# Two chosen-token layers with half of the rank comparisons, a moved gather and mask, and newly written orders for the last layer

## The reference, cut to what matters

```python
scores = jnp.einsum('btd,d->bt', hidden_states, w_router)
_, idx = jax.lax.top_k(scores, k)            # k = 128 of 1024
idx = jnp.sort(idx, axis=-1)
sel = hidden_states[b, idx]
x, pos = sel.reshape(S, D), idx.reshape(S)
...                                          # rms norm, q, k, v with biases, rope at pos
att = jnp.where(causal[None], att, jnp.finfo(att.dtype).min)
att = jax.nn.softmax(att, axis=-1)
...                                          # output projection, rms norm, gated MLP
gated = gate * processed + (1.0 - gate) * x  # gate = sigmoid(score)
output = hidden_states.at[b, idx].set(gated.reshape(B, k, D))
```

## Time and profile before

| | |
|---|---|
| median of 3 runs | 1503.42 us (1502.92 to 1507.25) |
| profiled execution, its own time | 1500.55 us |
| its span, first to last instruction | 1499.0 us |
| mean granted TensorE clock | 0.985 |
| PE busy | 1432.7 us (96%) |
| DVE, ACT, POOL busy | 1089.7, 1030.0, 680.9 us |
| f1 in the span | about 597 to 680 us |
| f2 | about 1147 to 1230 us |
| layer1 | about 1230 to 1499 us |

### The profile page before, as it was taken

The page is one execution under the profiler, slowest core; times in us unless marked ns, Lnnn a source line. Parts: engine busy times, 40 slices in busy tenths (PEclk is TensorE's granted clock), DMA queues, the critical chain, the costliest instruction groups (busy, mean ns, idle before and its releaser), DMA issues. The chain is left out here.

```text
span 1499.0 us, 23651 instructions
## 1 busy us (share of the span) xinstructions
PE 1432.7 (96%) x8460; PEld 1217.9 (81%) x8460; DVE 1089.7 (73%) x2447; ACT 1030.0 (69%) x2254; POOL 680.9 (45%) x816
## 2 busy tenths in 40 slices
PE   7899999999999998998999999999999997988899
PEld 6789898888989886786888888888897785766677
DVE  6989898989898976656766666766666749567643
ACT  4898989999898986465755655655654446675654
POOL 6676776676776555113433333343321112722233
PEclk9999999999999999999999999999999999899999
DMA  2000000000000000601000000000003314000000
GB/s 74 2 18 1 19 9 12 1 19 19 1 8 2 14 1 12 256 1 51 22 22 8 22 29 8 22 29 15 1 8 130 138 31 167 1 0 0 1 0 28
DMA packets 14339, 45.11 MB, mean 30 GB/s; under 512 B 3216, under 2 KB 3216, under 8 KB 12048
## 3 DMA queue, kind: packets, MB, share of 16 engines
q1 hardware_dynamic: 14224, 43.61, 8.1%
HBM read 42.55 MB, written 1.05 MB: 29 GB/s over the span
## 5 line engine op out<-in xcount | busy, mean ns | idle before, releaser
L386 POOL TENSOR_SCALAR a_prob<-a_prob,a_rowinv 128x128 f32<-128x128 f32 (+7 forms) x256 | 189.0, 753 | 132.1 <-DVE a_rowinv L380 131.9
L411 DVE TENSOR_TENSOR a_pT_lo<-ps,a_pT_hi 128x512 fp32r<-128x512 f32 (+3 forms) x384 | 194.8, 551 | 21.1 <-ACT a_pT_hi L403 19.4
L364 DVE CUSTOM_DVE_ANT_0 a_prob<-ps,a_mask 128x128 f32<-128x128 f32 (+7 forms) x256 | 187.0, 750 | 21.2 <-PE ps L149 20.9
L371 ACT ACTIVATE a_prob<-a_prob,a_negmax 128x128 f32<-128x128 f32 (+7 forms) x256 | 197.3, 778 | 2.2 <-DVE a_negmax L364 1.3
L386 POOL TENSOR_SCALAR b_prob<-b_prob,b_rowinv 128x128 f32<-128x128 f32 (+7 forms) x128 | 94.6, 751 | 199.6 <-DVE b_rowinv L380 199.5
L403 ACT ACTIVATE a_pT_hi<-ps 128x512 fp32r<-128x512 f32 (+3 forms) x384 | 167.3, 492 | 24.7 <-PE ps L344 15.4
L344 PE MATMUL ps<-ident,a_prob 128*128 128x128 f32 x1152 | 160.2, 275 | 7.0 <-DVE a_pT_lo L411 5.6
L371 ACT ACTIVATE b_prob<-b_prob,b_negmax 128x128 f32<-128x128 f32 (+7 forms) x128 | 99.6, 779 | 72.6 <-DVE b_negmax L364 71.8
L344 PEld LDWEIGHTS ps<-ident,a_prob 128*128 128x128 f32 x1152 | 130.0, 140 | 20.6 <-POOL a_prob L386 7.9
L149 PE MATMUL ps<-a_k_hi,a_q 128*128 128x512 f32 (+3 forms) x384 | 140.4, 373 | 1.9 <-DVE a_negmax L364 1.0
L355 PE MATMUL ps<-a_pT_hi,a_v 128*128 128x512 f32 (+3 forms) x384 | 131.2, 349 | 1.1 <-DVE a_pT_lo L411 0.6
(11 more groups left out here) (452 smaller groups left out, 4025.0 us busy)
## 6 DMA issues: line engine op xcount, KB each, us to landing
f_wq<-in_f_wq SPq DMA_DIRECT2D x2, 2048.0 KB, 9.0
f_wo<-in_f_wo SPq DMA_DIRECT2D x2, 2048.0 KB, 17.1
b_w_raw<-in_b_qk SPq DMA_DIRECT2D x16, 256.0 KB, 2.7
a_w_raw<-in_a_w SPq DMA_DIRECT2D x8, 384.0 KB, 3.2
a_vo<-in_a_o SPq DMA_DIRECT2D x8, 256.0 KB, 2.7
f_wk<-in_f_wk SPq DMA_DIRECT2D x2, 1024.0 KB, 10.8
f_wv<-in_f_wv SPq DMA_DIRECT2D x2, 1024.0 KB, 12.9
f_wg<-in_f_wg SPq DMA_DIRECT2D x2, 1024.0 KB, 19.7
```

The lines of the kernel that those rows point to most:

```text
L364: dve.tensor_tensor_reduce(slot(a, u), g.ps_flat[:, bank * HALF:bank * HALF + width], a.mask[:, N - width:], -1.0, -MASKED, ALU.add, ALU.m ...
L371: act.activation(prob, prob, ACT.Exp, bias=a.negmax[:, n:n + 1], scale=-1.0, accum_out=a.rowsum[:, n:n + 1]).then_inc(*g.exped.mark(a.tag, u))
L386: pool.tensor_scalar(prob, prob, a.rowinv[:, n:n + 1], 1.0, ALU.mult, ALU.mult).then_inc(*g.normed.mark(a.tag, u))
L411: dve.tensor_tensor(lo, src, fr(hi), ALU.subtract).then_inc(*g.lo.mark(a.tag, u, j0 // 4))
```

## The change

In `ffn`, a token of an early block is no longer compared with the blocks before it. Of a pair of tokens in different blocks one comparison is kept, and for blocks 0 to 4 (`F_ROWS` is 5) the missing count is worked out as the number of later tokens less the sum of the row, which ACT makes with accumulating copies (`held`); DVE subtracts and adds it to the ranks. The unread products become fewer (3, 2, 2, 2, 2, 1, 1, 0). The gather goes to bank 3 and runs between the products of `take` and `place`. The mask moves ahead of the rope factors. In the second half, the product for the gate goes ahead of `scores(2)`, `turn_prob(0)` ahead of `scores(3)`, and `turn_take` behind `out(3)`. Two of the copies of `h_tok` on ACT go behind the new copies. POOL gets an iota and two memsets more. In `layer1` the four strings are new; the steps are the same ones, counted by program.

```diff
+F_SPIN = (3, 2, 2, 2, 2, 1, 1, 0)
+F_ROWS = 5
+        f.unread = f.sq[:, :].rearrange("p b k q -> p (b k q)").bitcast(BF16)
...
-    pool.memset(f.upper[:], 1.0).then_inc(*done.mark(tag, "ones"))
+    pool.memset(f.lower[:], 1.0).then_inc(*done.mark(tag, "ones"))
+    pool.iota(f.later[:, 0:F_ROWS], pattern=[[-P, F_ROWS]], base=N - P, ...)
+    pool.memset(f.later[:, F_ROWS:TT], 0.0)
+    pool.memset(f.minus_b[:], -1.0)
...
 def ffn_beats(f, e, j):
-    own, hi = f.s_col[:, j:j + 1], (j + 1) * P
-    e.tensor_scalar(f.beats[j // 4][:, j % 4, 0:hi], f.s[:, 0:hi], own, None, ALU.is_lt)
-    if hi < N:
-        e.tensor_scalar(f.beats[j // 4][:, j % 4, hi:N], f.s[:, hi:N], own, None, ALU.is_le)
-    return e.scalar_tensor_tensor(f.ties[:, j], f.s[:, j * P:hi], own, f.upper[:], ALU.is_equal, ALU.mult)
+    own, lo = f.s_col[:, j:j + 1], j * P
+    e.tensor_scalar(f.beats[j // 4][:, j % 4, lo:N], f.s[:, lo:N], own, None, ALU.is_le)
+    if j > F_ROWS:
+        e.tensor_scalar(f.beats[j // 4][:, j % 4, F_ROWS * P:lo], f.s[:, F_ROWS * P:lo], own, None, ALU.is_lt)
+    return e.scalar_tensor_tensor(f.ties[:, j], f.s[:, lo:lo + P], own, f.lower[:], ALU.is_equal, ALU.mult)
...
-        for c in range(TT):
+        for c in range(min(j, F_ROWS), TT):
             t = mm(ranks[:, c:c + 1], f.beats[...], f.ones_b[:], False, j == TT - 1)
+    def gather(c):
+        for m in range(KT):
+            t = mm(bank[3][:, m * P:m * P + P], f.h_tok[:, c, m * P:m * P + P], fr(f.take[:, c]), ...)
     for c in range(TT):
         t = mm(bank[5][:, 0:4], f.take[:, c], f.place[:, c], c == 0, c == TT - 1)
+        if c % 2:
+            gather(c // 2)
     pe.wait_ge(*act.at(tag, "h_tok", 3))
-    for c in range(TT): ...   (16 products, mark xs)
+    gather(4)
+    gather(5)
     pe.wait_ge(*dve.at(tag, "own"))
     mm(bank[0][:, 0:P], f.own[:, 1:2]..., g.ident[:], True, True)   (mark h1)
+    gather(6)
+    gather(7)   (mark xs)
...
-    scores(2)
-    scores(3)
-    turn_prob(0)
-    turn_prob(1)
-    turn_take(0)
-    turn_take(1)
     (the product for the gate)
+    scores(2)
+    turn_prob(0)
+    scores(3)
+    turn_prob(1)
...
     out(3).then_inc(*done.mark(tag, "wo"))
+    turn_take(0)
+    turn_take(1)
...
+    for j in range(F_ROWS):                                       (ACT)
+        rest = f.beats[j // 4][:, j % 4, (j + 1) * P:N]
+        act.wait_ge(*dve.at(tag, "beats", j))
+        t = act.activation(f.unread[...], rest, ACT.Copy, accum_out=f.held[:, j:j + 1])
+    h_tok(2)
+    h_tok(3)
...
+    dve.wait_ge(*act.at(tag, "held"))
+    dve.tensor_tensor(f.later[:, 0:F_ROWS], f.later[:, 0:F_ROWS], f.held[:, 0:F_ROWS], ALU.subtract)
+    dve.wait_ge(*done.at(tag, "later"))
     dve.wait_ge(*pe.at(tag, "rank"))
-    dve.tensor_copy(f.rank[:], bank[2][:, 0:TT])
+    dve.tensor_tensor(f.rank[:], bank[2][:, 0:TT], f.later[:], ALU.add)
...
+    dve.wait_ge(*pe.at(tag, "others"))    (mask, moved from between turn(3) and turn(4) to behind h1)
+    dve.tensor_scalar(f.mask[:], bank[7][:, 0:P], f.own[:, 0:1], MASKED, ALU.is_gt, ALU.mult)
```

More of the change, by code:

```diff
@@ L1254, in ffn_pe @@
         t = mm(bank[5][:, 0:4], f.take[:, c], f.place[:, c], c == 0, c == TT - 1)
-    t.then_inc(*done.mark(tag, "own"))
+        if c == TT - 1:
+            t.then_inc(*done.mark(tag, "own"))
+        if c % 2:
+            gather(c // 2)
     pe.wait_ge(*act.at(tag, "h_tok", 3))
[L1257 to L1260, removed]
+    gather(4)
+    gather(5)
     pe.wait_ge(*dve.at(tag, "own"))
     mm(bank[0][:, 0:P], f.own[:, 1:2].broadcast_to([P, P]), g.ident[:], True, True).then_inc(*done.mark(tag, "h1"))
+    gather(6)
+    gather(7).then_inc(*done.mark(tag, "xs"))
     mm(bank[7][:, 0:P], f.own[:, 0:1].broadcast_to([P, P]), g.ident[:], True, True).then_inc(*done.mark(tag, "others"))
@@ L1415, in ffn_act, with h_tok @@
         act.activation(f.std1[:, ht], f.ratio[:, ht], ACT.Sqrt, bias=g.eps[:, 1:2]).then_inc(*done.mark(tag, "std1", b))
-    for t in range(4):
+    def h_tok(t):
         act.wait_ge(*pe.at(tag, "h_tok", t))
@@ L1420, in ffn_act @@
         x.then_inc(*done.mark(tag, "h_tok", t))
-        if t == 1:
-            for b, cc in halves():
-                act.wait_ge(*dve.at(tag, "s", b))
-                act.activation(f.inv_row[:, cc], bank[4 * b + 2], ACT.Copy).then_inc(*done.mark(tag, "inv", b))
+    h_tok(0)
+    h_tok(1)
+    for b, cc in halves():
+        act.wait_ge(*dve.at(tag, "s", b))
+        act.activation(f.inv_row[:, cc], bank[4 * b + 2], ACT.Copy).then_inc(*done.mark(tag, "inv", b))
+    for j in range(F_ROWS):
+        rest = f.beats[j // 4][:, j % 4, (j + 1) * P:N]
+        act.wait_ge(*dve.at(tag, "beats", j))
+        t = act.activation(f.unread[:, j * N - j * (j + 1) // 2 * P:][:, 0:N - (j + 1) * P], rest, ACT.Copy, accum_out=f.held[:, j:j + 1])
+    t.then_inc(*done.mark(tag, "held"))
+    h_tok(2)
+    h_tok(3)
     act.wait_ge(*g.f_loaded["bqk"].at(tag))
@@ L1455, in ffn_act @@
     act.wait_ge(*pe.at(tag, "xs"))
-    act.activation(f.xs[:, :].rearrange(FLAT), bank[4][:, 0:2 * P], ACT.Copy).then_inc(*done.mark(tag, "xs"))
+    act.activation(f.xs[:, :].rearrange(FLAT), bank[3][:, 0:2 * P], ACT.Copy).then_inc(*done.mark(tag, "xs"))
     for p, n in enumerate(F_ORDER):
@@ L1567, in ffn_dve @@
                                  ALU.mult).then_inc(*done.mark(tag, "h1", k))
+    dve.wait_ge(*pe.at(tag, "others"))
+    dve.tensor_scalar(f.mask[:], bank[7][:, 0:P], f.own[:, 0:1], MASKED, ALU.is_gt, ALU.mult).then_inc(*done.mark(tag, "mask"))
     dve.wait_ge(*pe.at(tag, "ropes"))
@@ L1608, in ffn_dve @@
     turn(3)
-    dve.wait_ge(*pe.at(tag, "others"))
-    dve.tensor_scalar(f.mask[:], bank[7][:, 0:P], f.own[:, 0:1], MASKED, ALU.is_gt, ALU.mult).then_inc(*done.mark(tag, "mask"))
+    most(0)
     turn(4)
-    most(0)
+    most(1)
     turn(5)
-    most(1)
     divide(0)
```

40 lines of the change are left out of this document (22 added, 18 removed).

## The result

The changed kernel takes 1491.28 us (median of 4 runs, 1489.25 to 1492.75), the kernel before 1503.17 in the same comparison (4 runs, 1500.84 to 1507.25). The ratio is 0.9917, with an interval of 0.99 to 0.9934: 12.5 us faster by the ratio, 11.9 by the medians. The forecast was 1487.1 with a range of 1479 to 1497. The profiled execution of the changed kernel has a span of 1491.5 us; it is the slowest of its four runs, and that of before is the fastest of its own, so the spans show only 7.5 of the 12 us.

A forecast was written before the change was run, and what follows sets the result against it. PE was taken to bound layer1 at its end, and a chain through DVE, PE and ACT the chosen-token layers. Terms of 9.5 us for both such layers and 6.8 for layer1 gave 16.3 us, so 1487.1, range 1479 to 1497.

The forecast's parts named there:

- Comparisons: Front of each chosen-token layer: fewer comparisons on DVE bring the ranks 2.4 us earlier, with ACT's accumulating copies hidden.
- What the mask held up: Chosen-token layers: an early mask removes PE's wait before scores(0) and the low clock; with the front, x1 comes 4.75 us earlier.
- Rival 2: PE's clock falls in the thinner comparisons and gather, costing 2 us for each layer: 1491; chance 0.12.
- Port: Start of layer1: two POOL splits moved behind the first ring step no longer slow DVE beside them; 2.6 us won.
- t1: layer1: the inverse of half 1 no longer waits for gate work behind a scan; 0.7 us won.
- middle: layer1 before out: five PE steps of half 2 fill a wait, against two more ACT table loads; 2.0 us won.
- n2: layer1's second norm: half 2's mean goes behind half 1's inverse, so up1 starts earlier; 2.5 us won.
- late: layer1, half 2's gates: ACT's loads around gelu 3 and gelu 4 against a removed wait; 1.0 us lost.
- Rival 1: layer1: the new orders give nothing, idle time only moves; 1494 us, chance 0.22.
- Rival 3: layer1: early waits shrink below what the clock needs to fall, 4 to 6 us come back; 1482 us, chance 0.12.
- Rival 4: layer1: ACT's seven loads, PE's rests and clock falls hold up out, 23 us; 1511 us; chance 0.06 slower, 0.06 no change.

The follow-up runs named there:

- Run 8: The kernel before with only the mask moved on DVE, to behind h1 instead of between turn(3) and turn(4): 1499.51 us.
- run 1: The change with the four old strings of layer1, so only the chosen-token layers are new: 1494.13 us.
- run 4: The change with POOL's whole old string in layer1: 1505.14 us.
- Run 5: The change with one stretch of ACT's string, in the gates of layer1's half 1, put back nearly to its old order: 1489.96 us.
- run 6: The change with PE's mean of half 2 again in front of the inverse of half 1's second norm: 1492.99 us.
- run 9: The change with layer1's old order on four engines from half 1's second norm on, keeping its inverse ahead of half 2's mean: 1489.29 us.
- run 10: The change with layer1's old order on four engines from the l norm's inverse to the second norm: 1493.65 us.
- run 3: The change with three unread products after every block of comparisons: 1489.10 us.
- run 11: The change with the old-order stretches of run 9 and run 10 together, and three unread products after each block but the last: 1494.26 us.
- run 12: The kernel of run 3 with 32 more unread products of 512 columns in front of half 1's out in layer1: 1487.93 us.
- run 7: The kernel of run 1 with the old comparisons and rank products and three unread products, without held: 1498.28 us.
- run 2: The kernel before with the four new strings of layer1: 1501.13 us.

## Why the prediction came out as it did

The forecast of 1487.1 was 4.2 us too low. The half that lies in the chosen-token layers was right to 0.1 us, but by luck: two errors of about 1 us a layer stand against each other. The half in layer1 was too large.

**Comparisons:** 2.4 us forecast, 2.36 measured. Right, with `held` hidden as said. The sum took for granted that PE keeps up with the faster comparisons; that holds only with the fewer unread products, which are 0.62 of the 2.36. The five copies on ACT took 3.6 us and not 4.2: the 768 columns cost 0.83, where the row of the exponentials had 0.94.

**What the mask held up:** 2.35 us of the 4.75 forecast, 3.37 measured. The mechanism was right: no wait before scores(0), clock 1.00 through the values. Run 8, the mask alone, gives 2.62. What was missed are two terms that the forecast put at nothing or left out. The gather was to give 0 and gives 0.5: half of it now stands between the `place` products, which went at DVE's pace, so the rope factors, xs and the keys come earlier. And "turns and most(0) follow each other" holds for the old order only: the diff also puts most(0) in front of turn(4), and ACT's last 0.43 us of waiting before the first exponential goes. Together they bring the first exponentials to 29.63 us and not 30.5. From there to `turned(1)` it took 7.86 us, forecast 7.9. `turn_take` behind out(3) cost nothing: from x1 of f2 to the first mean of layer1 it is 16.24 us before and after.

**Rival 2:** given a chance of 0.12 as a lasting state, it is true in some layers and not in others. Of the 14 chosen-token layers profiled with the new unread products (the change, runs 1, 4, 5, 6, 9 and 10) 4 have the fall, and it costs 3.23 us each, not 2. That makes 0.92 us a layer on average. So 11.5 us for both layers less 1.8 is 9.6, which is what run 1 measured. PE is busy for 2.9 of the 4 us from 3 to 7 us behind the first comparison in all 14, with and without the fall, so what decides lies outside these instructions. With three unread products PE is busy for 3.9 of these 4 us and none of 6 layers has the fall (runs 3, 11, 12). At 4 in 14 that would still come about by chance once in eight times, so that these products prevent it is likely and not shown.

**layer1** was forecast at 6.8 us. The timed value is 2.6 (1.1 to 4.1). By the profiles it is 4.2: the mean of the four with the old strings (before, runs 1, 7, 8) against the four with the new (the change, runs 2, 3, 12). us from the first mean of layer1 to reciprocals of half 1's norms on DVE, and to the end of the span:

| | r | t1 | l | n2 | end |
|---|---|---|---|---|---|
| before | 8.8 | 38.0 | 83.5 | 129.7 | 268.7 |
| old strings, mean | 8.8 | 39.1 | 85.3 | 131.75 | 270.7 |
| the change | 6.4 | 34.0 | 81.6 | 129.2 | 266.9 |
| new strings, mean | 6.4 | 34.0 | 81.4 | 128.75 | 266.55 |

The old ones scatter by 4.2 us in the last column and the new ones by 2.4, and before's profile was the shortest of its kind; the gap between 2.6 and 4.2 is not settled beyond that. Stretch by stretch:

- To the first norm (r): 2.4 us won that the forecast did not have. The new strings also put half 1's std and reciprocal ahead of half 2's squares, which neither the list of the new order nor the prediction has. Before, one of these squares took DVE 2.29 us instead of 0.69, beside POOL's split of `r`, right in front of that reciprocal.
- r to t1: 2.8 us won. *Port* and *t1* were to give 2.6 and 0.7; run 4 measured 2.1 for the port, which leaves 0.6 for the order.
- t1 to l: 1.3 us lost, forecast 0 (46.1 us in the mean of the old strings, 45.3 to 46.9; 47.5 in the new ones, 46.7 to 48.8). The term *port* had the displaced splits lie beside a DVE that is half idle. In the rows, DVE's new order has a chain of five operations of two columns there (`softplus`), and behind it the `l_work` that PE waits for. Before, four of the five take 0.17 us each and nothing waits. DVE and PE of the change, then DVE, POOL and PE of run 4:

```profile
1277.84 1.26 DVE L1849 TENSOR_SCALAR l_softplus<-l_softplus 128x2 f32<-128x2 f32 x1
1279.13 1.20 DVE L1851 TENSOR_SCALAR l_softplus<-l_softplus 128x2 f32<-128x2 f32 x1
...
1281.64 1.03 PE L2007 MATMUL ps<-l_h_hi,l_t_gate 128*128 128x512 f32 x2 [1.86 <-DVE l_work L2203]
```

```profile
1281.45 3.27 DVE L1853 TENSOR_SCALAR l_softplus<-l_softplus 128x2 f32<-128x2 f32 x1
1281.28 3.42 POOL L1889 TENSOR_TENSOR l_up_lo<-l_raw_up,l_up_hi 128x1536 fp32r<-128x1536 f32 x1
...
1285.83 1.22 PE L2007 MATMUL ps<-l_h_hi,l_t_gate 128*128 128x512 f32 x2 [4.79 <-DVE l_work L2203]
```

  An operation of 0.17 us takes 3.27 when it starts behind the split of `up`, and it ends with it. The nine profiles with the new order of POOL here have PE's wait, 1.8 to 2.2 us, run 4 has 4.79, and none of the four with the old strings has it. No run moved the chain alone, so that it is the whole of the loss is not shown.
- l to n2: 0.8 us lost, forecast 2.0 won (old strings 46.2 to 47.2 us, new ones 47.0 to 47.6). This is the step that failed, *middle*: the last high part before `out` was to come 2.0 us earlier. Counted from the l norm's reciprocal it comes 38.1 to 38.6 us behind with the new strings and 38.0 to 38.5 with the old, so nothing was won there. Of the wait of 2.9 us only 1.0 to 1.5 were won, for the gates' first load stands at 17.3 to 17.8 us instead of 18.8. From there to `out`'s first high part ACT has seven loads of 1.283 us instead of five, 2.6 us more, and in the change it works from 1323.98 to 1342.44 us without a pause. Run 5, with five loads but DVE waiting 11.24 us, was no better. From the last high part to the last product of `out` it is 2.2 to 2.6 us with the old strings and 3.4 with the new, at the low clock. Runs 10 and 11 show that, behind the new t1 stretch, the new middle is still some 2 to 3.5 us better than the old one. What makes the pair together no better than the old pair is not settled.
- n2 to the end: 1.15 us won, forecast 1.5. *n2* was 2.5 (measured 2.6 to up1) and right. *late* was -1.0, and what is left for it here is -1.45; but run 9, with the late order put back, is 0.4 us longer and not shorter. So *late* has no price of its own either, and that the sum fits is in part luck.

**Rival 1** (orders give nothing) and the forecast were both off: the truth of 1491.3 lies between 1487.1 and 1494. **Rival 3** did not happen: the mean clock of the 200 us is 0.93 as before. **Rival 4** had its place right and its price wrong: seven loads, a rest of 8.5 us and the low clock through `out`. But the 23 us of loss did not come: five of the seven loads there were in the old order too, and PE has nothing to be late with until ACT's high parts are there. What is left of it is the 0.8 us of the middle. No drain stands in the rows: ACT has seven loads of 1.28 us there, and most are followed by their activation within 0.02 us. By the Trainium skill ("ScalarE: Activation LUTs", § What ACT_TABLE_LOAD costs) the loads would have been an estimated 18.6 us more on ACT; the trace has 15 us more busy time on ACT in the whole span, `held` in both layers and 9 us of loads included.

## What to carry to other kernels

Take a hand-written schedule of several engines as one thing: putting back one of four strings cost 13.9 us, and putting back a stretch on one engine left another waiting 11 us. Cost a chain from a diff line by line, for a small swap left out (the gather, most(0), the first norm, the two-column chain) was here as large as the terms that were worked out with care. Where work is moved, look at what stands beside it in its new place. When work is thinned out, look at what it did for the clock: a saving of 5.7 us loses 3.2 of them in 4 of 14 layers, and which layers these are can't be seen from one profile. The thinner unread products save 0.62 us a layer here and the falls cost 0.92 on average.

## What the runs showed of the hardware

- The same instructions at the same distances got a clock of 1.00 in 10 layers and of 0.50 in 4, after a stretch in which PE was busy for 2.9 of 4 us. The lower level lasted some 7 us and cost 3.23.
- A rest of 8.5 us before `out` was followed by the low clock, and rests of 1.11 and 2.25 us behind a filled stretch had it fall inside the second one. Keeping PE busy for 7.46 us just before did not prevent it.
- DVE's add of x takes 0.69 us alone and 1.60 beside a POOL split, in one kernel against another at the same place. Ten of ten such adds and comparisons end 0.55 us behind the end of the split beside them, and an operation of two columns takes 3.27 us instead of 0.17 beside a split of 3.42. The Trainium skill, "SBUF — State Buffer", § SBUF: two separate sides, tells of a port that one of the two holds for its whole instruction while the other is blocked. The trace agrees: what is lost is about the part of the split that was still left, and 0.91 us beside a split of 2.08 looks like less than a full block, as the prediction had it, only against the split's whole length.
- ACT's accumulating copies from 896 down to 384 columns take 0.95, 0.83, 0.72, 0.61 and 0.51 us as steps, with the readout included: 0.11 us for each 128 columns, as forecast, from a lower start.
